# A four-layer Mamba stage on one core: scans over pairs of channel tiles, decays in SBUF, each tile begun by a column of its own

## The reference, cut to what matters

```python
# x: (4, 576, 256); L_ = 4 layers, DI_ = 512 channels, DS_ = 16 states
xz = einsum('bsd,ed->bse', x, ip_w); xi, z = split(xz)
xi = silu(conv(xi) + cb)                       # depthwise, 4 taps
dt, Bm, Cm = split(xi @ xp_w); dt = softplus(dt @ dtp_w + dtp_b)
dA  = exp(dt[..., None] * A)                   # decay
dBu = dt[..., None] * Bm[:, :, None, :] * xi[..., None]
h   = da * h + dbu                             # step over the sequence, per channel and state
y   = sum over states of h * c
y = (y + xi * Dp) * silu(z);  out = y @ op_w   # added to x
```

## Time and profile before

| | us |
|---|---|
| median of 3 runs | 4412.1 (4411.99 to 4414.61) |
| profiled execution | 4420.25 |
| its span | 4418.1 |
| PE, busy | 3755.0 (85%) |
| DVE, busy | 3056.4 (69%) |
| ACT, busy | 2354.4 (53%) |
| POOL, busy | 2114.1 (48%) |

### The profile page before, as it was taken

The page is one execution under the profiler, slowest core; times in us unless marked ns, Lnnn a source line. Parts: engine busy times, 40 slices in busy tenths (PEclk is TensorE's granted clock), DMA queues, the critical chain, the costliest instruction groups (busy, mean ns, idle before and its releaser), DMA issues. The chain is left out here.

```text
span 4418.1 us, 51543 instructions
## 1 busy us (share of the span) xinstructions
PE 3755.0 (85%) x16536; PEld 1943.5 (44%) x16536; DVE 3056.4 (69%) x4176; ACT 2354.4 (53%) x4473; POOL 2114.1 (48%) x2144
## 2 busy tenths in 40 slices
PE   8999999999988688888888888887888768888787
PEld 4444444444444244444444444444444434344443
DVE  4426435364353499999999999999999956474653
ACT  2334323233231477767777677776777626354462
POOL 1003112031120378877888877787788833132230
PEclk9999999999999799999999999999999979999999
DMA  3110000000000533223332233322432120000000
GB/s 147 39 57 1 1 19 1 10 10 1 15 1 0 150 84 87 75 81 94 91 87 72 78 94 87 86 83 78 112 87 80 46 79 1 11 1 11 1 6 5
DMA packets 135961, 228.47 MB, mean 52 GB/s; under 512 B 19280, under 2 KB 118864, under 8 KB 126864
## 3 DMA queue, kind: packets, MB, share of 16 engines
q1 hardware_dynamic: 135696, 225.20, 17.3%
HBM read 192.55 MB, written 32.60 MB: 51 GB/s over the span
## 5 line engine op out<-in xcount | busy, mean ns | idle before, releaser
L2052 POOL TENSOR_TENSOR m_db<-m_u,m_bb 128x512 f32<-128x512 f32 (+1 forms) x1280 | 1466.1, 1165 | 418.6 <-DVE m_hh L2004 415.4
L2004 DVE TENSOR_TENSOR_SCAN m_hh<-psum,m_kept,m_db 128x512 f32<-128x512 f32 (+1 forms) x1024 | 1196.2, 1202 | 29.9 <-ACT m_kept L1821 23.3
L1800 ACT ACTIVATE psum<-m_dt,m_am 128x512 f32<-128x512 f32 (+1 forms) x1280 | 817.7, 644 | 394.2 <-DVE m_hh L2004 390.6
L1729 PE MATMUL psum<-cst,m_hh 128*128 128x128 f32 x4608 | 659.7, 284 | 324.8 <-DVE m_yt L2018 227.6
L1729 PEld LDWEIGHTS psum<-cst,m_hh 128*128 128x128 f32 x4608 | 524.3, 144 | 753.4 <-DVE m_yt L2018 440.1
L1739 PE MATMUL psum<-m_ys,cst 128*128 128x512 f32 x1024 | 545.5, 615 | 0.0
L2018 DVE SCALAR_TENSOR_TENSOR m_yt<-psum,m_bc,m_yt 128x512 f32<-128x512 f32 x600 | 437.9, 730 | 41.1 <-PE psum L1729 40.0
L798 POOL TENSOR_SCALAR a_pr<-a_pr,a_ri 128x512 f32<-128x512 f32 x256 | 174.1, 694 | 609.5 <-DVE a_ri L612 609.5
L1812 ACT ACTIVATE m_ys<-psum,m_bc 128x512 f32<-128x512 f32 x512 | 344.7, 673 | 25.5 <-PE psum L1729 24.0
L798 POOL TENSOR_SCALAR c_pr<-c_pr,c_ri 128x512 f32<-128x512 f32 x256 | 172.5, 694 | 364.6 <-DVE c_ri L731 364.6
L652 ACT ACTIVATE a_pr<-psum,a_mx 128x512 f32<-128x512 f32 x256 | 173.7, 684 | 268.2 <-DVE a_mx L602 268.2
(11 more groups left out here) (242 smaller groups left out, 5624.2 us busy)
## 6 DMA issues: line engine op xcount, KB each, us to landing
m_bb<-b_rows SPq DMA_DIRECT2D x48, 1024.0 KB, 4.7
m_xr<-x_line SPq DMA_DIRECT2D x128, 192.0 KB, 4.0
m_bb<-b_rows SPq DMA_DIRECT2D x32, 768.0 KB, 4.5
m_xr<-x_line SPq DMA_DIRECT2D x128, 160.0 KB, 3.6
m_xr<-x_line SPq DMA_DIRECT2D x128, 128.0 KB, 3.3
m_xr<-x_line SPq DMA_DIRECT2D x128, 96.0 KB, 3.5
x_line<-m_xc SPq DMA_DIRECT2D x32, 192.0 KB, 2.8
m_wa<-w_in SPq DMA_DIRECT2D x4, 1376.0 KB, 7.4
```

What stands on the lines that cost most here:

```text
L1729: mm = nc.tensor.transpose(s[:, e * P:(e + 1) * P], hh[:, n % 2, e, t * P:(t + 1) * P], ident)
L1800: nc.scalar.activation(bank(DECAY[u % len(DECAY)])[:, 0:w], dt[:, g % 2, e, 0:w], ACT.Exp, scale=am[:, layer_of(g) % 2, e * DS + n:e * DS ...
L2004: nc.vector.tensor_tensor_scan(hh[:, n % 2, e, 0:w], bank(DECAY[u % len(DECAY)])[:, 0:w], db[:, u % 4, 0:w], kept[:, n, e:e + 1] if g % NI ...
L2052: nc.gpsimd.tensor_tensor(db[:, u % 4, 0:w], us[:, g % 2, e, 0:w], bb[:, at % 2, n % 4, 0:w], ALU.mult).then_inc(pool_done, pr.pool.step(f ...
```

## The change

A round is now two units: DVE scans two channel tiles (`GE` = 2) in one instruction of 2 x (w + 1) elements. The decays go to a ring `da` of `RING` = 4 pairs in SBUF, the inputs to a ring `db` of as many; both scan inputs are then in SBUF. Each tile begins with an extra column, in which the decay is 0 and the input is the state carried over, or 0; it restarts the recurrence, and the pointer to `kept` as start value is gone. POOL writes that column with an instruction of its own in front of each product (a copy out of `kept`, or in two steps of a layer's first item a memset), and makes the product of a pair in one instruction. ACT still makes one decay for each tile, and zeroes the decays' column only when the width changes. ACT and POOL work `AHEAD` = 6 units ahead.

The three banks that the decays had go to the others: the two kinds of transposes have two banks each, the side jobs two. The order of transposes and additions in `outputs` is changed; the added positions of state n no longer wait for the state after. Room in SBUF comes from buffers that now serve two uses (`sq` is `xn`, `xc` is `yg`, `yp` lies in `us`) with waits that go with it, and from `bb`, which holds two states a half where it held four: B is fetched in 160 transfers where there were 80, issued between the writes and gathers of the next item. Softplus and the products u come in other slots.

```diff
-            xc = sb("xc", [P, NE, BANK])
-            sq = sb("sq", [P, ND, BANK])
+            sq = xn
-            bb = sb("bb", [P, 2, 4, BANK])
-            db = sb("db", [P, 4, BANK])
-            hh = sb("hh", [P, 2, NE, BANK])
+            bb = sb("bb", [P, 2, 2, BANK])
+            GE, RING = 2, 4
+            da = sb("da", [P, RING, GE * (BANK + 1)])
+            db = sb("db", [P, RING, GE * (BANK + 1)])
+            hh = sb("hh", [P, 2, NE * (BANK + 1)])
+            xc = yg
-            DECAY, SUMS, TURN_D, TURN_P, SIDES = (0, 1, 2), (3, 4), 5, 6, (7,)
+            SUMS, TURN_D, TURN_P, SIDES = (3, 4), (5, 0), (6, 1), (7, 2)
-            DTP, BCT, SOFT, OUT, Z = 37, 44, 45, (58, 61), (46, 49, 52, 55)
+            DTP, BCT, SOFT, OUT, Z = 37, 44, 43, (58, 61), (46, 49, 52, 55)
+            U, CUT, AHEAD = (47, 50, 53, 56), 57, GE * (RING - 1)
...
+            def row(buffer, slot, g, tiles):
+                w = width(g) + 1
+                return buffer[:, slot, 0:tiles * w].rearrange("p (e s) -> p e s", s=w)
+
+            def sums_out(g, k):
+                return us[:, g % 2, k, :]
...
# sync: chunk
-                        at = 4 * g + c
+                        at = 8 * g + c
                         if at >= 2:
-                            i, j = divmod(at - 2, 4)
-                            sp.wait_ge(pool_done, pr.pool.at(f"{i} db {4 * j + 3} {NE - 1}"))
+                            i, j = divmod(at - 2, 8)
+                            sp.wait_ge(pool_done, pr.pool.at(f"{i} db {2 * j + 1} {NE - GE}"))
...
+                        chunk(g, 2)
                         if more:
                             write(g + 1, 0)
                             write(g + 1, 1)
                             gather(g + 1, 0)
+                        chunk(g, 3)
+                        if more:
                             write(g + 1, 2)
                             gather(g + 1, 1)
                             write(g + 1, 3)
-                        chunk(g, 2)
+                        chunk(g, 4)
                         if more:
                             gather(g + 1, 2)
                             gather(g + 1, 3)
+                        chunk(g, 5)
+                        if more:
                             state_rows(g + 1)
-                        chunk(g, 3)
+                        chunk(g, 6)
+                        chunk(g, 7)
...
# tensor: outputs
-                        if e == 0:
-                            turn(g, n, d[0])
-                            turn(g, n, p[0])
-                        if e == 2 and len(p) > 1:
-                            turn(g, n, p[1])
-                        if e == 2 and len(d) > 1:
-                            turn(g, n, d[1])
-                        if e == 3:
-                            add(g, n, 0)
+                        if e < len(p):
+                            turn(g, n, p[e])
+                        if e < len(d):
+                            turn(g, n, d[e])
+                        if e >= 2 and e - 2 < len(p):
+                            add(g, n, e - 2)
...
# scalar: decay
-                        if u >= len(DECAY):
-                            i, m, f = units[u - len(DECAY)]
-                            act.wait_ge(dve_done, pr.dve.at(f"{i} scan {m} {f}"))
-                        nc.scalar.activation(bank(DECAY[u % len(DECAY)])[:, 0:w], dt[:, g % 2, e, 0:w], ACT.Exp,
+                        slot = u // GE % RING
+                        if e % GE == 0:
+                            if u >= GE * RING:
+                                i, m, f = units[u - GE * RING]
+                                act.wait_ge(dve_done, pr.dve.at(f"{i} scan {m} {f}"))
+                            if n < GE * RING // NE and (g == 0 or width(g - 1) != w):
+                                nc.scalar.activation(row(da, slot, g, GE)[:, :, 0:1], none[:, 0:GE].unsqueeze(2), ACT.Copy)\
+                                    .then_inc(act_done, pr.act.step())
+                        nc.scalar.activation(row(da, slot, g, GE)[:, e % GE, 1:1 + w], dt[:, g % 2, e, 0:w], ACT.Exp,
...
# vector: scan, and in yd a wait
+                                    if post + 2 < ITEMS:
+                                        dve.wait_ge(x_written[e % 2], written(post + 2, e))
...
-                        dve.wait_ge(act_done, pr.act.at(f"{g} da {n} {e}"))
+                        dve.wait_ge(act_done, pr.act.at(f"{g} da {n} {e + GE - 1}"))
                         dve.wait_ge(pool_done, pr.pool.at(f"{g} db {n} {e}"))
-                            if g % NI:
-                                dve.wait_ge(act_done, pr.act.at(f"{g - 1} keep {n}"))
-                        nc.vector.tensor_tensor_scan(hh[:, n % 2, e, 0:w], bank(DECAY[u % len(DECAY)])[:, 0:w],
-                                                     db[:, u % 4, 0:w], kept[:, n, e:e + 1] if g % NI else 0.0,
+                        at, slot = e * (width(g) + 1), u // GE % RING
+                        nc.vector.tensor_tensor_scan(hh[:, n % 2, at:at + w], da[:, slot, 0:w], db[:, slot, 0:w], 0.0,
                                                      ALU.mult, ALU.add)\
...
# gpsimd: state_input
-                        nc.gpsimd.tensor_tensor(db[:, u % 4, 0:w], us[:, g % 2, e, 0:w], bb[:, at % 2, n % 4, 0:w],
+                        to = row(db, slot, g, GE)
+                        if g % NI:
+                            pool.wait_ge(act_done, pr.act.at(f"{g - 1} keep {n}"))
+                            nc.gpsimd.tensor_copy(to[:, :, 0:1], kept[:, n, e:e + GE].unsqueeze(2)).then_inc(pool_done, pr.pool.step())
+                        elif n < GE * RING // NE:
+                            nc.gpsimd.memset(to[:, :, 0:1], 0.0).then_inc(pool_done, pr.pool.step())
+                        nc.gpsimd.tensor_tensor(to[:, :, 1:1 + w], us[:, g % 2, e:e + GE, 0:w],
+                                                bb[:, at % 2, n % 2, 0:w].unsqueeze(1).to_broadcast([P, GE, w]),
                                                 ALU.mult).then_inc(pool_done, pr.pool.step(f"{g} db {n} {e}"))
```

More of the change, by code:

```diff
@@ L1475, in build @@
             sides = SideBanks(pr, bank, SIDES)
-            turn_d, turn_p = Ring(pr, bank, [TURN_D]), Ring(pr, bank, [TURN_P])
+            turn_d, turn_p = Ring(pr, bank, TURN_D), Ring(pr, bank, TURN_P)
             units = [(g, n, e) for g in range(ITEMS) for n in range(DS) for e in range(NE)]
@@ L1723, in turn @@
                             s, freed = turn_p.take(f"{g} ht {n} {t}", pr.act, f"{g} ys {n} {t}")
-                        if t == 0:
-                            pe.wait_ge(dve_done, pr.dve.at(f"{g} scan {n} {NE - 1}"))
+                        if t == tiles_p(g)[0]:
+                            pe.wait_ge(dve_done, pr.dve.at(f"{g} scan {n} {NE - GE}"))
                         if freed:
@@ L1760, in _ @@
                         pe.wait_ge(*sides.emptied[b])
-                    before = earlier = None
+                    before = None
                     for g, n in steps:
@@ L1770, in _ @@
                                 outputs(*before, e)
-                            if earlier and e == 1 and len(tiles_p(earlier[0])) > 1:
-                                add(*earlier, 1)
                             side(NE * n + e, *neighbours(g))
-                        before, earlier = (g, n), before
+                        before = (g, n)
                     for e in range(NE):
                         outputs(*before, e)
[L1777 to L1781, removed]
+                    sides.lend(TURN_D, (dve_done, pr.dve.at(f"{ITEMS - 1} y {LAST} {tiles_d(ITEMS - 1)[-1]}")))
                     for q in range(NE * DS):
@@ L1811, in scaled @@
                         act.wait_ge(pe_done, pr.pe.at(f"{g} ht {n} {t}"))
-                        nc.scalar.activation(ys[:, k, :], bank(TURN_P), ACT.Identity,
+                        nc.scalar.activation(ys[:, k, :], full(f"{g} ht {n} {t}"), ACT.Identity,
                                              scale=bc[:, g % 2, t, DR + DS + n:DR + DS + n + 1], bias=0.0)\
@@ L1819, in keep @@
                             return
-                        act.wait_ge(dve_done, pr.dve.at(f"{g} scan {n} {NE - 1}"))
-                        nc.scalar.activation(kept[:, n, :].unsqueeze(2), hh[:, n % 2, :, width(g) - 1:width(g)], ACT.Copy)\
+                        act.wait_ge(dve_done, pr.dve.at(f"{g} scan {n} {NE - GE}"))
+                        nc.scalar.activation(kept[:, n, :].unsqueeze(2), row(hh, n % 2, g, NE)[:, :, width(g):width(g) + 1], ACT.Copy)\
                             .then_inc(act_done, pr.act.step(f"{g} keep {n}"))
@@ L1830, in side @@
                                         act.wait_ge(pe_done, pr.pe.at(f"{post - 1} yf {NE - 1}"))
-                                    nc.scalar.activation(yp[:, k, :], bank(SUMS[k]), ACT.Copy)\
+                                    nc.scalar.activation(sums_out(post, k), bank(SUMS[k]), ACT.Copy)\
```

(32 more changed lines are left out.)

42 lines of the change are left out of this document (19 added, 23 removed).

## The result

The changed kernel takes 5096.1 us (median of 4 runs, 5093.91 to 5098.22), the kernel before 4413.35 beside it. The ratio is 1.155, 95% interval 1.153 to 1.157: it is 683 us slower. 5130 was predicted. The profiled execution took 5093.91 us, its span is 5091.8.

A forecast was written before the change was run, and what follows sets the result against it. DVE, 95% busy in the Mamba stage, was taken as the bound. Rounds 2548 + columns 77 + other products 167 + taps 13 = 2805 us against 2081, +724 on the median 4412.1: 5136, said as 5130; range 4580 to 5340.

The forecast's parts named there:

- What bounds the kernel: Mamba stage before: DVE, busy 1970.6 of 2081.4 us, sets the pace; PE, POOL and ACT follow.
- The exclusion: Mamba stage: a scan with both inputs in SBUF and a POOL product cannot run together; chance 0.76.
- The size of a round: One pair scan plus one POOL product, less 0.23 us given back: 4.41 us at 512, 3.34 at 384; 2548 us together.
- The columns: POOL's 512 copies of the extra column before products, 0.15 us each: 77 us, ends 0 and 102.
- POOL's other products: Mamba stage: 96 products of 1.27 us and 64 of 1.00 now add to the path: 167 us.
- the shared way: Access to SBUF that a scan with two SBUF inputs and a POOL instruction reading SBUF can only have in turn.
- The sum: Mamba stage: 2548 + 77 + 167 + 13 = 2805 us against 2081, +724.
- Waits costed at nothing: Waits added for shared buffers name work ending tens of slots ahead; ACT's decays are six units ahead: nothing.
- Edits costed at nothing: B fetched in halves, waits for shared buffers and ACT's decays written to SBUF (18 us on an idle engine): nothing.
- The rival without exclusion: Scans with two SBUF inputs run beside POOL; DVE stays the bound, 127 us of scans and waits saved: 4230; chance 0.13.
- Sharing by turns: Rival: scan's second input holds SBUF access for 1.04 of each element's 2.086 ns; stage +183, 4595 us; chance 0.09.
- the first rule in the prediction: Trainium skill: of a two-SBUF-input DVE instruction and a GpSimd SBUF reader, the second is blocked throughout; stage 147 us longer.

The follow-up runs named there:

- e4: Kernel before, with 384-wide items' position tiles split one to DVE and two to ACT and PE, 128 additions fewer on DVE: 4407.7 us, ratio 0.9985.
- e1: Kernel before, with only the decays moved from PSUM to three SBUF buffers, scans still single: 5037.5 us, ratio 1.142.
- e5: As e1, but the scan reads its second input from PSUM bank 0 instead of POOL's product, which is still made: 4412.8 us, ratio 1.000.
- e2: Changed kernel, with POOL's product of a pair replaced by a memset of the same elements, so it writes without reading: 4419.9 us, ratio 1.002.
- e3: Changed kernel without POOL's 512 column copies, the state carried over between items left out: 5036.7 us, ratio 1.141.
- e7: As e2, with PE's additions in PSUM cut from 512 columns to 128: 4365.4 us, ratio 0.989.
- e8: Kernel before, with PE's 1024 additions in PSUM cut from 512 columns to 128: 4389.6 us, ratio 0.995.

## Why the prediction was right, point by point

- *What bounds the kernel.* Right that DVE is the fullest engine and that POOL, PE and ACT wait for it; wrong that it alone sets the pace. PE's stream, 1748 us busy of 2081, reads like 16% of room, yet e4 took 4% off DVE, gave it to PE and ACT, and gained 0.15%. It did not hurt the forecast, because the exclusion sets a slower pace than any engine alone.
- *The exclusion.* Shown on both sides: e1 makes most of the loss with this part alone, e5 takes it away by moving one input, e2 by taking POOL's reading away. One DVE instruction of 1.62 us at 46.26 us was enough to see it in advance. The copies at a layer's change were the second sign; the same line now has a maximum of 1693 ns beside a product of 1.82 us. They have one input each, so two inputs are not what it takes for every DVE instruction.
- *The size of a round.* 4.41 and 3.34 us worked out, 4.31 and 3.23 measured without a column's copy (e3). The 0.23 us given back a round came from one pair of instructions; what is given back is the fixed parts of both, 0.14 + 0.19 = 0.33 us for pairs and 0.20 + 0.19 = 0.39 for single scans with `kept`. With 0.23 for it, e1's round of 512 was expected at 2.31 us and takes 2.15; over all rounds that is some 180 us too much, of which other time (below) took 50 back.
- *The columns.* 77 us, measured 59 by e3.
- *POOL's other products.* 167 us for 160 products in line for the shared way. Not measured by itself. That they queue is shown: 2658 ns for 1277 at yg. A round of 512 with a yg product in it takes 5.66 us in the median against 4.45, 1.21 more, where 1.15 was taken.
- *The sum.* +724 predicted for the stage, +679 measured. Here is an estimate by the elements alone, with the rates of the prediction. The scans of the stage are 591,104 elements of 2.086 ns and the products 589,824 of 2.125 ns, 2486 us together where the prediction has 2548. With 59 for the columns and, by the same rate, some 163 for the 152 other products that lie in the stage and the taps (167 + 13 in the prediction), that is 2708; 52 us are left that no term names. e1 comes out alike: 2646 by its elements, 2699 measured. So the terms were about 97 us too high and 52 us of other time were put at nothing. That 5130 came within 34 us of 5096 is in part the luck of these two.
- *Waits costed at nothing.* The prediction puts ACT's waits at nothing, with its decays six units ahead. At twelve changes of item they now stand 8.5 to 12.7 us behind the memset of `dt` that POOL makes after its last product u (the first line has eight of them); before the change no wait of ACT in the stage was over 5 us. At seven of them a scan waits 6.5 us for ACT in turn. It cost little that can be seen, as POOL worked on meanwhile, and e1, which has no such order, has as much time left over.

```profile
ACT m_da L1815 <- POOL m_dt L2131: 98.3, 8, 12.7
1751.33 0.72 ACT L1815 ACTIVATE m_da<-m_dt,m_am 128x512 f32<-128x512 f32 x1 [12.69 <-POOL m_dt L2131]
1752.28 3.67 DVE L2021 TENSOR_TENSOR_SCAN m_hh<-m_da,m_db 128x1026 f32<-128x1026 f32 x1 [6.46 <-ACT m_kept L1836]
```

- *Edits costed at nothing.* Halved B, shared buffers and ACT's 32 ns: not measured one by one. e2 has all of them together with the gain of the pairs and ends 0.2% above before; e3 has them too and ends where e1 does, which has none of them but the 32 ns. They are not seen at this size, and a cost that a gain offsets is not ruled out.
- *The rival without exclusion* was mis-sized. I had it at 4230, from 127 us of scan time and 55 of waits. DVE's busy time fell by 50 us in e2 (1970.6 to 1920.1): single scans overlap their neighbour by more than I took (two of 384 fill 1.92 us where their durations add up to 2.00), and the products that POOL still makes lengthen the scans beside them, 69 ns in the mean over all, 44 us. The waits did not go, they became waits for PE (86.6 us). With POOL's 640 products turned into writes the changed kernel is as fast as before (e2, 4420), not 4% faster.
- *Sharing by turns* is out: in the timeline POOL's product has its own length, 2.36 us, with the whole wait in its partner, and 4595 us is far from 5096.

So the change had little to win in DVE's stream either: with a lighter PE on both sides, e7 is 24 us below e8. And pairing does not help once the exclusion rules: without the copies it takes 5036.7 us (e3), and single scans take 5037.5 (e1). Pairs save fixed parts, and by the sums above these cost nothing in the shared regime.

The version that moves 128 additions off DVE in the kernel before (e4) is the fastest of those that leave nothing out, 0.15% under it (interval 0.06% to 0.24%).

## What to carry to other kernels

Before an input of a hot DVE instruction moves from PSUM to SBUF, count its tensor inputs in SBUF: a scan with one ran beside POOL, with two it and POOL's reading instructions took turns, and the cost was the sum of both engines' elements. A copy from SBUF to SBUF took turns with one input already, so the count is no rule for every instruction. Look for the one place in the old trace where such an instruction already meets POOL; a duration that is sometimes longer, by up to the length of the other's instruction, is the sign, since no view of waits names it. And before an engine is called the bound, take some work off it: here 4% less for DVE brought 0.15%.

## What was not expected of the hardware

- The shared way is held for the elements, not for the instruction: 2.15 us a round of a 512 scan and a 512 product, which is 512 x (2.086 + 2.125) ns, though the two take 1.27 us each alone. By the first rule in the prediction, a wait for the whole of the other, it would be 2.54; the measurement decides.
- A two-column copy of 0.18 us cost 0.12 us a time in the total and 0.14 in an undisturbed round, although it lies in front of a product that has to wait for the same scan.
- Cutting 322 us of PE's busy time in additions left PE with 173 us less (1748 to 1575): the granted clock fell from 0.96 to 0.88, and the unchanged transposes took 86 us more.
